# Perceiver layer on one core: experts unrolled with deeper rings, last three head pairs ordered by batch

## What is computed

```
# self-attention, 16 heads of 64
qkv = data @ W_qkv + b_qkv                                # 256 -> 3 x 1024
attention = softmax(einsum('nqhd,nkhd->nhqk', q, k) / 8)
x = x + einsum('nhql,nlhd->nqhd', attention, v).reshape(n, l, 1024) @ W_out + b_out
# experts, on xf = layernorm(x)
scores = sigmoid(xf @ gate_w.T)                           # 16 experts; 4 of them per token, from the
                                                          # best 2 of 4 groups, weights cw (normed, x 2.5)
y = einsum('nei,ne,ehi->nh', silu(xf @ Wg) * (xf @ Wu), cw, Wd)   # every expert on every token
y = y + silu(xf @ Ws_g.T) * (xf @ Ws_u.T) @ Ws_d.T        # shared part, 2 x 128 hidden
x = x + xf + y
```

## Time and profile before

| | us |
|---|---|
| three executions | 627.2, 633.71, 636.61 (median 633.71) |
| the profiled execution | 633.59 |
| its span, first to last instruction | 631.8 |
| PE busy | 582.3 (92%) |
| DVE busy | 465.1 (74%) |
| ACT busy | 410.4 (65%) |
| POOL busy | 118.3 (19%) |

### The profile page before, as it was taken

One profiled execution on the slowest core, in us unless ns is written; L12 is line 12 of the kernel. 1 busy time (PEld: TensorE's weight loads), 2 busy tenths in 40 slices (PEclk: granted clock), 3 DMA queues, 4 the chain that ended last, 5 costly groups with the idle time before them and its releaser, 6 DMA issues.

```text
span 631.8 us, 11892 instructions
## 1 busy us (share of the span) xinstructions
PE 582.3 (92%) x4512; PEld 322.6 (51%) x4512; DVE 465.1 (74%) x685; ACT 410.4 (65%) x834; POOL 118.3 (19%) x150
## 2 busy tenths in 40 slices
...
PEclk9999999999999999999999999899999997898998
...
DMA packets 11381, 21.99 MB, mean 35 GB/s; under 512 B 1858, under 2 KB 6724, under 8 KB 10308
## 3 DMA queue, kind: packets, MB, share of 16 engines
q1 hardware_dynamic: 11332, 21.31, 10.0%
...
HBM read 20.78 MB, written 0.52 MB: 34 GB/s over the span
## 4 chain that ended last, share of the span: by engine, by line
PE 73%; DVE 15%; ACT 5%; issue 4%; DMA 2%; POOL 1%; SPq 0%; DVEq 0%
PE bank L574 21%; PE bank L585 16%; DVE mxp L1170 11%; PE pairS L838 6%; PE pairS L663 5%; PE bank L855 4%; PE pairS L713 3%; ACT Pb L962 2%; PE bank L738 2%; PE bank L724 2%; PE bank L517 1%; PE pairS L824 1%; PE pairS L568 1%; DMA ctx<-ctxT 1%; PE pairS L593 1%
## 5 line engine op out<-in xcount | busy, mean ns | idle before, releaser
L1170 DVE TENSOR_REDUCE mxp<-pairS 128x1 f32<-128x1024 f32 x256 | 306.7, 1221 | 36.1 <-PE pairS L568 34.9
L962 ACT ACTIVATE Pb<-bank 128x512 f32<-128x512 f32 x512 | 274.0, 599 | 56.4 <-PE bank L574 43.8
L574 PE MATMUL bank<-qparts,kparts 64*128 64x512 f32 x512 | 189.7, 453 | 12.9 <-DVE mxp L1170 6.4
L568 PE MATMUL pairS<-kparts,qparts 64*128 64x512 f32 x512 | 189.3, 455 | 2.8 <-DVE mxp L1170 2.0
L585 PE MATMUL bank<-Pb,V 128*32 128x256 f32 x2048 | 151.6, 389 | 1.2 <-ACT accS L948 1.2
L574 PEld LDWEIGHTS bank<-qparts,kparts 64*128 64x128 f32 x512 | 78.6, 184 | 117.2 <-ACT Pb L962 75.5
L585 PEld LDWEIGHTS bank<-Pb,V 128*32 128x32 f32 x2048 | 46.5, 108 | 74.4 <-issue 47.5
L568 PEld LDWEIGHTS pairS<-kparts,qparts 64*128 64x128 f32 x512 | 78.0, 184 | 7.6 <-DVE mxp L1170 2.5
L383 POOL CAST mparts<-mneg 128x8 fp32r<-128x8 f32 x16 | 3.2, 199 | 368.6 <-DVE mneg L1178 368.6
L1241 DVE TENSOR_REDUCE smx<-pairS 128x2 f32<-128x512 f32 x32 | 21.8, 686 | 32.7 <-PE pairS L713 32.7
L398 POOL TENSOR_TENSOR Pb<-Pb,srd 128x512 f32<-128x512 f32 x32 | 33.3, 1041 | 66.6 <-DVE srd L1246 66.3
...
## 6 DMA issues: line engine op xcount, KB each, us to landing
...
```

The costliest lines, as they stand in the source:

```text
L568: last = mm(dst[:, i * 512:(i + 1) * 512], qparts[rows, at:at + P], kparts[c // NCH][rows, k:k + 512], start=True, stop=True)
L574: mm(dst[:], kparts[g // NCH][rows, s * P:(s + 1) * P], qparts[rows, g * CW:(g + 1) * CW], start=True, stop=True).then_inc(exp_filled, 1)
L962: A(PT[:, s % 8, :], src, ACT.Exp, scale=1.0 / np.sqrt(XD)).then_inc(exp_free, 1)
L1170: nc.vector.reduce_max(mxp[:, c % 2 * NBLK + blk, kp:kp + 1], pairS[n % 2][:], AX).then_inc(max_free, 1)
```

## The change

1. **Order of the attention's cycles** (`CYCLES`). Pairs 0 to 4 run as before, both batches of a pair after each other (cycles 0 to 9). Pairs 5, 6 and 7 run by batch: 10, 11, 12 are batch 0 and 13, 14, 15 are batch 1, so batch 0 is complete after cycle 12. Pairs 6 and 7 are needed earlier, so cycles 10 and 11 hold two fills each (q and k) and 12 to 15 none. Buffers `kTb`, `qb`, `aT` and `wO` go from two to three. From unit 24 on, the transposed units alternate between bank 0 and `half[0]`.
2. **The seam.** The norm of batch 0 is cut into `norm_begin`, three `norm_root` rounds and `norm_end`, which lie between the instructions of cycles 14 and 15. PE transposes batch 0 into ACC before the last `out_product`, batch 1 into MISC. The high and low parts are taken from PSUM straight (`high_x` on ACT, `x_low` on DVE); `xnT` and POOL's L415 go.
3. **Experts 0 and 1** are split like the others and their down products add up in PSUM, so `add_expert(0)` goes. `gate` takes `xh` and `xl`: 8 fp32 products per batch instead of 4.
4. **Three experts in flight.** up(e) is followed by down(e-2); the up results have three pairs of banks, the down results one pair instead of two. Experts 0 to 2 do their batch 0 half, then their batch 1 half.
5. **Weights.** Rings of 4 (`wU`) and 3 (`wD`) with buffers of their own. The up weights of experts 0 to 3 are cast and split in cycles 11 to 14, the first down weight after cycle 15. In each turn e ACT does silu(e), high_up(e+4), high_hidden(e), high_down(e+1), and POOL low_hidden(e), low_up(e+4), low_down(e+1). All loops are unrolled.
6. **The end.** The low part of the last expert's hidden values is made in two halves; `down` signals each batch by itself, and `add_expert` waits for each.

```diff
+BY_BATCH = 3
+CYCLES = ([(p, b) for p in range(NPAIR - BY_BATCH) for b in range(B)]
+          + [(p, b) for b in range(B) for p in range(NPAIR - BY_BATCH, NPAIR)])
...
-    for n in range(2, NCYC - 2):
+    for n in range(2, NCYC - 6):
         at[n] = [("k" if n % 2 else "q", n // 2 + 1)]
+    for p in range(NPAIR - 2, NPAIR):
+        at[NCYC - 6 + p - (NPAIR - 2)] = [("q", p), ("k", p)]
...
+        after_fills = bank[0][:], half[0]
+        def pT_bank(u):
+            return after_fills[u % 2 if u // 2 > LAST_FILL else 0]
...
# gpsimd, in the attention's loop and after it
+                if NCYC - 5 <= n < NCYC - 1:
+                    low_up(n - (NCYC - 5))
+                if n == NCYC - 1:
+                    low_down(0)
+            for e in range(NE - 1):
+                low_hidden(e, slice(0, B * L), 1)
+                if e + RU < NE:
+                    low_up(e + RU)
+                low_down(e + 1)
+            for b in range(B):
+                low_hidden(NE - 1, slice(b * L, (b + 1) * L), 1)
...
# tensor
             out_product(n - 2)
             attn_T(2 * n - 1)
             attn_out(n - 1)
+            norm_batch_T(5, 0, ACC)
             out_product(n - 1)
...
+            pe.wait_ge(xl_done, 3)
+            up(0, first)
+            up(1, first)
+            norm_batch_T(6, 1, MISC)
+            up(2, first)
             gate(0)
+            pe.wait_ge(xl_done, 4)
             gate(1).then_inc(gate_ps, 1)
+            for e in range(RG):
+                up(e, second)
+            down(0)
+            for e in range(RG, NE):
+                up(e)
+                down(e - 2)
+            down(NE - 2)
+            down(NE - 1)
...
# in down(e)
+                for b in range(B):
+                    if e >= 2:
+                        pe.wait_ge(down_read, 2 * (e - 2) + b + 1)
...
# scalar
+            for e in range(NE):
+                silu(e)
+                if e + RU < NE:
+                    high_up(e + RU)
+                high_hidden(e)
+                if e + 1 < NE:
+                    high_down(e + 1)
...
# vector, in the loop over cycles
+                if n == NCYC - 1:
+                    norm_root(both[0], 1)
...
                 reciprocals(2 * n + 1)
+                if n == NCYC - 2:
+                    dve.wait_ge(wO_used, LAST_OF[0] + 1)
+                    add_batch(0, ACC[:])
+                    norm_begin(both[0])
+                if n == NCYC - 1:
+                    norm_root(both[0], 1)
+            pT_move(2 * NCYC - 2)
+            norm_root(both[0], 1)
+            norm_end(both[0])
+            pT_move(2 * NCYC - 1)
+            x_low(3, ACC[:])
+            dve.wait_ge(wO_used, LAST_OF[1] + 1)
+            add_batch(1, MISC[:])
...
# vector, experts: hidden(0) after the group minima and maxima of the router, hidden(1) and hidden(2) after its
# penalties (L1355), hidden(3) and add_expert(1) after the best four, then the weights cw, then:
+            hidden(4)
+            for e in range(2, NE):
+                add_expert(e)
+                if e + 3 < NE:
+                    hidden(e + 3)
```

437 lines of the change are left out of this document (183 added, 254 removed).

## The result

The changed kernel's median is 628.0 us (625.13 to 632.0, 19 runs). The kernel before was timed beside it, in 19 runs, at 636.03 us (627.2 to 637.91). The ratio of the two is 0.9925, with a 95% interval of 0.9903 to 0.9947: 0.75% less, about 4.8 us, well inside what counts as no change at 2%. Over all runs of the first timing the medians are 8.0 us apart and the means 6.5. The forecast was 626.0 us, 1.2% under its base. The time is within the range; the gain is smaller than forecast, and the interval leaves the forecast ratio of 0.988 out.

A forecast was written before the change was run, and what follows sets the result against it. PE, with DVE in between, bounds the self-attention, PE the steady experts; at the seam nothing overlaps. Down(0) at 547.0 plus 67.0 stream, 4.0 stalls, 2.6 clock, 3.6 end and 1.8 outside the span gave 626.0 us, range 618 to 634.

The forecast's parts named there:

- Part 1: Attention from cycle 10: the new order costs 1.7 us, cycle 15 starting at 517.5 where it was 515.85.
- Part 2: From cycle 15 to the first down product: 28.6 us, plus 0.9 for Newton rounds beside POOL, down(0) at 547.0.
- Part 3: PE's stream from down(0) on: 18 downs of 1.43 and 15 ups of 2.75, 67.0 us, to 614.0.
- Part 4: Stalls in PE's expert stream, before down(1), down(3) and the last down: 4.0 us in sum, to 618.0.
- (a): Before down(1): hidden(1) stands behind the router's ranks, held back by POOL; its low part is 2.0 us late.
- (c): Last down: waits 0.4 us instead of 2.2, each half waiting for the add before it.
- Part 5: Low clock after idle PE, in its expert stream: 2.6 us that PE cannot hide, bounds 0 and 6, to 620.6.
- Part 6: End: 3.6 us behind the last down instead of 4.3, span 624.2, plus 1.8 outside it, 626.0.
- A: Early stage: DVE slips between POOL's instructions, down(1) and down(3) find their data, clock stays up: 618.9; chance 0.25.
- B: Attention: POOL's four low parts get ahead of normalizations, up to 5.2 us more, 631.2; chance 0.10.
- C: Seam, up(2) to up(5): the clock stays low, 12.6 us more, 638.6; chance 0.08.
- D: Scalar table switch at the seam: about 1.38 us of draining added, time 627.4; chance 0.05.

The follow-up runs named there:

- e7: Changed kernel with the attention by pair as before and the low part of batch 0's input made right behind its norm: 628.06 us, ratio 0.9911.
- e15: Changed kernel with attention by pair, early low input part, own banks for last-but-one down, fifth up weights' low part later; timed again: 624.18 us, ratio 0.9843.
- e3: Changed kernel with the last but one down product in a bank pair of its own: 628.0 us, ratio 0.9901.
- e4: Changed kernel with POOL's low part of each up weight from expert 4 on one place later: 626.82 us, ratio 0.9868.
- e5: Changed kernel with only two experts in flight from the sixth expert on: 628.34 us, ratio 0.993.
- e13: Changed kernel with 16 instead of 32 router products, leaving out the low part of the router's input: 625.02 us, ratio 0.9896.
- e14: Changed kernel as it is, timed and profiled once more: 626.89 us, ratio 0.9909 to the kernel before.
- e16: Changed kernel with the first half of the router's products ahead of the first half of up(2): 627.47 us, ratio 0.9905.
- e2: Changed kernel with batch 0's first Newton round moved behind the last copy of cycle 15's loop: 628.33 us, ratio 0.9933.
- e6: Changed kernel with the first four up weights and first down weights split behind the attention instead of inside it: 634.45 us, ratio 1.002.
- e8: Changed kernel with Newton rounds later, own banks for the last but one down, and fifth up weights' low part later: 626.3 us, ratio 0.9879.
- e9: Changed kernel with 26 more products on PE, results unread, in its waits in the last cycle and before batch 1's transposes: 626.75 us, ratio 0.9882.

## Why the prediction was right, and where it was wrong

**The place and the mechanism of the gain: right. Its size: wrong.** From cycle 10 to the end of the span the kernel before takes 142.9 to 143.2 in three profiles, the changed one 136.17 and 134.39; the forecast was 135.3. That is 6.8 to 8.8 us less, against 7.6. Of the whole kernel 4.8 us (0.75%) and, in the second timing, 5.8 us (0.91%) came by the ratios, where 7.7 (1.2%) were forecast.

**Part 1: right for the cycles, not for their start.** Cycle 15 at 28.2, forecast 28.6; fills moved out of half-hidden places cost 1.3 us. That the whole order by batch would not be worth these was not asked, and e7 and e15 show it. Cycle 10 itself was taken over at 488.94 and came 1.06 us later (below).

**Part 2: mis-sized, by 0.4 to 2 us** (down(0) 58.1 forecast, 58.47 and 60.13 measured). The rounds cost on the path what I took, 0.9: L1095 takes 0.88 too much twice, but the second lies beside `attn_out(14)`. The Trainium skill, SBUF — State Buffer, section "SBUF: two separate sides", says that the loser fully blocks for the whole instruction. The rows agree to 0.02 us: 520.02 and 520.00, 523.36 and 523.34. What the step lacked is the price of the 3.18 us in which PE waits for this: in the last cycle `attn_out(14)` at 1.98 instead of 1.08, the transposes at 1.05 instead of 0.60. In the other profiles that keep this idle the clock falls there too (e3, e4, e5, e13, e14 and e16 have 1.97 or 1.98); in those with an idle of 1.71 or 2.66 it doesn't (e2, e6, e8). The length alone does not decide it, since in the kernel before a low clock follows waits of 1.8. With the full clock there (e9) the transposes of batch 1 come at 46.54, and from them to down(0) it is 10.69 us at full clock (e14): 57.2 together, an estimate. So the rest of the sum was some 0.9 too long, and the low clock ahead of down(0), which stood at nothing in this part, took 1.2 us in e14 and 2.9 in the first profile.

**Part 3: right.** 67.0 us at 4.18 each; e5 shows that the ring of three has nothing to do with it.

**Part 4:** (a) down(1) 1.56 us, forecast 2.0, the mechanism shown by e4. In the changed kernel L1341, which takes 0.18 us alone, stands beside POOL's low hidden values (548.64 to 549.96):

```profile
548.71 1.28 DVE L1341 TENSOR_TENSOR Pb<-Pb 128x12 f32<-128x12 f32 x1
```

(b) down(3) 1.34, forecast 1.6. (c) was mis-sized: 0.86 + 0.41 instead of 0.4. I counted the wait for hidden values, but add_expert(16) cannot start before hidden(17), and down(16) stands behind add_expert(15) in the single pair of banks. e3 takes the waits away and wins 0.8 of the 1.3.

**Part 5: the place wrong.** I put 2.6 us of low clock behind down(0). No profile of the changed kernel has any there up to 600 us: from down(0) to the end of the last down it is 72.3, forecast 73.6. The low clock lies ahead of down(0), and the 2.6 come near its 1.2 to 2.9 us by luck.

**Part 6: the adds right** (3.69 from the last down to the end of the span, forecast 3.6), **the time outside the span wrong.** I carried over 1.8 us. In 86 runs of the kernel before, timed beside the variants, it is 1.78 on the mean, in the 19 of the changed one 2.45. So 0.67 us of the gain is given back where no profile looks. Every variant of the changed kernel has 2.4 to 2.6; which instruction brings it was not tried.

**The step that failed.** It is the sizes of terms, and above all those that I carried over as if they could not move. The first profile took 628.5 us, 2.5 more than the sum of 626.0, and this is made of: 1.06 more at the start of cycle 10 (part 1); 2.0 more up to down(0) (part 2, the low clock that it left out); 1.25 less from there to the end of the last down, since of the 6.6 us that parts 4 and 5 put on top of 67.0 only 5.4 came (4.2 of them the waits, the rest mostly PE's slower start behind them); 0.1 more behind it; 0.6 more outside the span (part 6). For e14, 626.61 us, it is 0.7, 0.4, minus 1.3, 0 and 0.8. So the two that stand in both are the time outside the span and the start of cycle 10, and neither has to do with the stages that I reasoned about. Cycle 10 starts at 488.87 in the first profile of the kernel before, but at 489.72 and 504.0 in its others, and between 488.2 and 494.2 in the twelve profiles of the order by batch, only once earlier than 488.87. The step of part 6 that took one profiled execution and the median of three runs to "compare directly" made the gain 7.7 us out of this: the profile that the sum started from had an early cycle 10, and the runs of the kernel before spread over 10 us.

**How large the gain is, the record leaves open within some microseconds.** Over 31 runs the changed kernel's span follows the granted clock: 628.2 to 629.5 us at 0.983, 621.8 to 622.7 at 0.996, some 0.5 us per 0.001. Before goes along: 629.0 to 632.0 at 0.984, 627.3 to 629.2 at 0.989. At an equal 0.986 the spans are 628.6 to 631.5 and 625.5 to 626.1: 4.2 us between the middles. But this takes away too much: the low stretches that the change removes are part of what raises the mean clock from 0.980 (86 runs) to 0.989 (31 runs). The medians over all runs differ by 8.0 and 6.1 us in the two timings, the means by 6.5 and 5.5, the ratios by 0.75% and 0.91%.

**The rivals.** A, the covered stage, fell: the waits before down(1) and down(3) that it took away are there. B, POOL's low parts ahead of normalizations, fell: cycles 12 to 14 are as forecast, and cycle 15 comes at 28.19 without the low parts (e6) as at 28.20 with them. The low parts hurt DVE instead. C, the long low clock, did not come in the changed kernel, but in e6: 13 us of low clock while PE is busy, and 5.3 us lost by it. So what I held for it, "from 534 to 536 the clock stayed at 0.50 while PE was busy", does happen over longer stretches. D fell: in e14 the load starts at 543.24 and the first silu at 544.53, 1.29 us later, with nothing else between. The Trainium skill, ScalarE: Activation LUTs, section "What ACT_TABLE_LOAD costs", adds about 1.38 us of draining; no row here shows it.
